# Weights loaded in contiguous parts with a later down load, and two float32 convolutions turned into float32r

## The reference, cut to what matters

```python
y = irfft(rfft(u, n=1024) * rfft(K, n=1024))[..., :512] + u * D[:, None]   # per row and channel
y = y * (arange(512) < length[:, None])
gate_out = fake_quant_linear(y, gate_w)      # 512 -> 1376, input rounded to FP8 e4m3 and back
up_out = fake_quant_linear(y, up_w)          # 512 -> 1376
hidden = silu(gate_out) * up_out
out = x + fake_quant_linear(hidden, down_w)  # 1376 -> 512, hidden rounded to FP8 e4m3 and back
```

## Time and profile before

| what | value |
|---|---|
| median of 3 runs | 311.52 us (311.35 to 312.45) |
| the profiled execution | 311.96 us, of which the trace's span is 310.2 us |
| PE busy | 298.6 us (96% of the span) |
| DVE busy | 216.1 us (70%) |
| ACT busy | 181.4 us (58%) |
| POOL busy | 40.4 us (13%) |
| granted TensorE clock | full in every slice |

### The profile page before, as it was taken

One profiled execution on the slowest core, in us unless ns is written; L12 is line 12 of the kernel. 1 busy time (PEld: TensorE's weight loads), 2 busy tenths in 40 slices (PEclk: granted clock), 3 DMA queues, 4 the chain that ended last, 5 costly groups with the idle time before them and its releaser, 6 DMA issues.

```text
span 310.2 us, 5071 instructions
## 1 busy us (share of the span) xinstructions
PE 298.6 (96%) x1833; PEld 171.1 (55%) x1833; DVE 216.1 (70%) x441; ACT 181.4 (58%) x248; POOL 40.4 (13%) x109
## 2 busy tenths in 40 slices
PE   1999999999999999999999999999999999999995
PEld 0457764755466555755556555655456554644443
DVE  6979699887756886678765886668764857453444
ACT  4926397386655567475755748466663646544640
POOL 4031000031001400022001400014001400140010
PEclk9999999999999999999999999999999999999999
DMA  6879999700705625074613726073001750060028
GB/s 199 194 189 229 298 238 314 294 4 0 270 2 85 188 71 200 2 136 137 227 43 56 190 41 254 0 135 135 3 1 21 150 237 0 10 128 0 2 41 230
DMA packets 14016, 38.43 MB, mean 124 GB/s; under 512 B 1470, under 2 KB 6558, under 8 KB 11052
## 3 DMA queue, kind: packets, MB, share of 16 engines
q1 hardware_dynamic: 8412, 26.61, 24.8%
q0 software_dynamic: 5584, 11.57, 21.5%
HBM read 33.93 MB, written 15.81 MB: 160 GB/s over the span
## 4 chain that ended last, share of the span: by engine, by line
PE 93%; DVE 3%; DMA 2%; issue 0%; SPq 0%
PE gate_ps L670 22%; PE up_ps L670 22%; PE down_ps L593 19%; PE y_ps L577 13%; PE y_ps L558 4%; PE y_ps L573 2%; PE gate_ps L643 2%; PE up_ps L643 2%; PE y_ps L611 2%; PE down_ps L711 2%; PE down_ps L611 2%; PE y_ps L711 1%; DMA toep<-kpad_scratch 1%; DMA prm<-in_params 1%; PE up_ps L623 1%; PE down_ps L517 1%
## 5 line engine op out<-in xcount | busy, mean ns | idle before, releaser
L977 DVE SCALAR_TENSOR_TENSOR hv<-sil,fac,up_ps 128x512 f32<-128x512 f32 (+1 forms) x88 | 64.7, 736 | 76.3 <-PE up_ps L670 44.1
L445 ACT ACTIVATE sil<-gate_ps,fac 128x512 f32<-128x512 f32 (+1 forms) x88 | 59.6, 677 | 97.7 <-PE gate_ps L670 79.5
L670 PE MATMUL gate_ps<-yq,wg 128*128 128x512 bf16 (+3 forms) x344 | 82.3, 362 | 0.0
L670 PE MATMUL up_ps<-yq,wu 128*128 128x512 bf16 (+3 forms) x344 | 82.3, 362 | 0.0
L593 PE MATMUL down_ps<-wd,hq 128*128 128x512 bf16 (+1 forms) x264 | 68.2, 380 | 0.0
L670 PEld LDWEIGHTS up_ps<-yq,wu 128*128 128x128 bf16 (+1 forms) x344 | 32.9, 98 | 35.7
L670 PEld LDWEIGHTS gate_ps<-yq,wg 128*128 128x128 bf16 (+1 forms) x344 | 32.4, 98 | 35.4 <-issue 0.5
L419 ACT ACTIVATE hq<-hv 128x1024 uint16<-128x1024 uint16 (+1 forms) x41 | 42.5, 1037 | 0.0
L410 ACT ACTIVATE yq<-yv 128x1024 uint16<-128x1024 uint16 x32 | 33.6, 1050 | 8.6 <-DVE yv L954 8.6
L577 PE MATMUL y_ps<-xh,th 128*128 128x512 f32 (+2 forms) x78 | 37.3, 478 | 0.6 <-issue 0.6
L593 PEld LDWEIGHTS down_ps<-wd,hq 128*128 128x128 bf16 (+1 forms) x264 | 23.0, 98 | 24.6 <-issue 6.0
(11 more groups left out here) (171 smaller groups left out, 273.9 us busy)
## 6 DMA issues: line engine op xcount, KB each, us to landing
xt<-in_xT SPq DMA_DIRECT2D x8, 1024.0 KB, 4.8
out<-in_x SPq DMA_DIRECT2D x7, 1024.0 KB, 5.3
out<-res POOLq DMA_DIRECT2D x7, 1024.0 KB, 7.7
toep<-kpad_scratch SPq DMA_DIRECT2D x6, 1024.0 KB, 7.5
toep<-kpad_scratch SPq DMA_DIRECT2D x8, 256.0 KB, 4.1
wd<-in_down POOLq DMA_DIRECT2D x1, 1280.0 KB, 18.8
xt<-in_x SPq DMA_DIRECT2D x1, 1024.0 KB, 7.3
out<-xt SPq DMA_DIRECT2D x3, 256.0 KB, 3.8
```

The lines of the kernel that those rows point to most:

```text
L445: nc.scalar.activation(sil[b][0:w, 0:cols], gate_ps[b][0:w, 0:cols], ACT.Silu, scale=fac[0:w, S_GATE:S_GATE + 1]).then_inc(silu_done, 1)
L670: mm = nc.tensor.matmul(ps[b][0:w, cols], wt[:, k, c * P:c * P + w], yq[par][:, version, k, cols], start=(k == 0), stop=(k == LB - 1))
L977: v.scalar_tensor_tensor(hv[c // 2 % 3][0:w, c % 2, 0:cols], sil[b][0:w, 0:cols], fac[0:w, S_UP:S_UP + 1], up_ps[b][0:w, 0:cols], ALU.mult ...
```

## The change

It has two parts. First, the gate and up weights get three tiles each in place of one (`wg[0]` to `wg[2]`), and the arrays in memory are laid out part by part, so that each partition's share of a part is one run: 1024, 1536 or 2944 float32 values in place of four runs of 256, 384 or 736. The down weights are laid out by partition too, so that ten runs of 512 values become one of 5120, and their load waits for block 2's Toeplitz rows (`conv_in[0]`) instead of block 1's fourth channel (`toep_first[7]`). Second, the third and fourth channel of block 0 are convolved by a new function `conv_low_taps_last` in float32r, from the pair of tiles `xh[1]`, `xl[1]`, `th[1]`, `tl[1]`; it takes the products with `tl` last. The casts and subtractions that this needs are put ahead of `code_y` on ACT and around the first `scale_y` on DVE.

```diff
+WEIGHT_PARTS = ((0, EARLY), (EARLY, MIDDLE), (MIDDLE, I))
...
-        wg = sb("wg", [P, LB, I], BF16)
-        wu = sb("wu", [P, LB, I], BF16)
+        wg = [sb(f"wg{i}", [P, LB, hi - lo], BF16) for i, (lo, hi) in enumerate(WEIGHT_PARTS)]
+        wu = [sb(f"wu{i}", [P, LB, hi - lo], BF16) for i, (lo, hi) in enumerate(WEIGHT_PARTS)]
...
+        def load_weights(eng, wt, w_d, i):
+            lo, hi = WEIGHT_PARTS[i]
+            return eng.dma_start(wt[i][:].rearrange("p k n -> p (k n)"), w_d[:, LB * lo:LB * hi])
...
-            pool.dma_start(wg[:, :, MIDDLE:], wg_d[:, :, MIDDLE:]).then_inc(weights_in, 16)
-            pool.dma_start(wu[:, :, MIDDLE:], wu_d[:, :, MIDDLE:]).then_inc(weights_in, 16)
-            pool.wait_ge(toep_first[2 * HB - 1], 16)
-            pool.dma_start(wd[:, 0:CH - 1, :],
-                           wd_d[0:(CH - 1) * P, :].rearrange("(k p) n -> p k n", p=P)).then_inc(down_in, 16)
-            pool.dma_start(wd[0:TAIL, CH - 1, :], wd_d[(CH - 1) * P:I, :]).then_inc(down_in, 16)
+            load_weights(pool, wg, wg_d, 2).then_inc(weights_in, 16)
+            load_weights(pool, wu, wu_d, 2).then_inc(weights_in, 16)
+            pool.wait_ge(conv_in[0], 16)
+            pool.dma_start(wd[:, 0:CH - 1, :].rearrange("p k n -> p (k n)"),
+                           wd_d[:, 0:(CH - 1) * L]).then_inc(down_in, 16)
+            pool.dma_start(wd[0:TAIL, CH - 1, :], wd_d[0:TAIL, (CH - 1) * L:]).then_inc(down_in, 16)
...
+            high_x_first(0, 1)
+            high_taps_first(0, 1)
             code_y(0, 0, 0)
             code_y(0, 0, 1)
             code_y(0, 0, 2)
-            high_x_first(1)
+            high_x_first(1, 1)
             code_y(0, 0, 3)
-            high_taps_first(1)
+            high_taps_first(1, 1)
...
+            def conv_low_taps_last(g, h):
+
+                pair, q = h // 2, h % 2
+                pe.wait_ge(x_split, splits_to(g, pair))
+                pe.wait_ge(taps_high, splits_to(g, pair))
+                pe.wait_ge(yv_done, HB * g + h - 1)
+                for taps, xs in ((th, xh), (th, xl), (toep, xt), (tl, xh)):
+                    if taps is tl:
+                        pe.wait_ge(taps_split, splits_to(g, pair))
+                    for d in (3,) if taps is toep else (0, 1, 2):
+                        cols, rest = slice(d * P, (d + 1) * P), slice(0, L - d * P)
+                        ch = (g, h) if taps is toep else (pair, q)
+                        last = nc.tensor.matmul(y_ps[q][:, d * P:L], taps[ch[0]][:, ch[1], cols], xs[ch[0]][:, ch[1], rest],
+                                                start=(taps is th and xs is xh and d == 0), stop=(taps is tl and d == 2))
+                last.then_inc(y_ready, 1)
...
-            for h in range(HB):
-                conv_whole(0, h)
+            conv_whole(0, 0)
+            conv_whole(0, 1)
+            conv_low_taps_last(0, 2)
+            conv_low_taps_last(0, 3)
             k_of(2)
...
+            low_x(0, 1)
             scale_y(0, 0)
+            low_taps(0, 1)
             scale_y(0, 1)
```

More of the change, by code:

```diff
@@ L200, in at_least, with splits_to @@
                 eng.wait_ge(s, v)
+        def splits_to(g, pair):
+            return 1 if isinstance(g, int) and g == 0 else 2 * (g - 1) + pair + 1
         def k_in_bank(i, half):
@@ L219, in high, with weights_of @@
             return ap.bitcast(U16).rearrange("p a (b s) -> p a b s", s=2)[:, :, :, 1]
+        def weights_of(wt, k, c):
+            i = 0 if c * P < EARLY else 1 if c * P < MIDDLE else 2
+            lo = c * P - WEIGHT_PARTS[i][0]
+            return wt[i][:, k, lo:lo + width(c)]
+        def load_weights(eng, wt, w_d, i):
+            lo, hi = WEIGHT_PARTS[i]
+            return eng.dma_start(wt[i][:].rearrange("p k n -> p (k n)"), w_d[:, LB * lo:LB * hi])
         def yq_of(par, h):
@@ L530, in warm @@
                 for n in range(count):
-                    nc.tensor.matmul(y_ps[n % 2][:], wg[:, 0, 0:P], wg[:, 0:2, 0:EARLY], start=True, stop=True)
+                    nc.tensor.matmul(y_ps[n % 2][:], wg[0][:, 0, 0:P], wg[0][:, 0:2, :], start=True, stop=True)
             pe.wait_ge(unit_in, 32)
@@ L566, in conv @@
                 if distances[0] == 0:
-                    at_least(pe, x_split, 2 * (g - 1) + pair)
-                    at_least(pe, taps_split, 2 * (g - 1) + pair)
+                    at_least(pe, x_split, splits_to(g, pair))
+                    at_least(pe, taps_split, splits_to(g, pair))
                     at_least(pe, yv_done, m - 1)
@@ L622, in by_channel @@
                         for k in range(LB):
-                            mm = nc.tensor.matmul(ps[c][:, cols], wt[:, k, c * P:(c + 1) * P],
+                            mm = nc.tensor.matmul(ps[c][:, cols], weights_of(wt, k, c),
                                                   yq[0][:, version, k, cols], start=(k == 0), stop=(k == LB - 1))
@@ L669, in slots @@
                                 for k in range(LB):
-                                    mm = nc.tensor.matmul(ps[b][0:w, cols], wt[:, k, c * P:c * P + w],
+                                    mm = nc.tensor.matmul(ps[b][0:w, cols], weights_of(wt, k, c),
                                                           yq[par][:, version, k, cols], start=(k == 0), stop=(k == LB - 1))
@@ L1137, in by_k, with by_chunk @@
     def by_k(w):
-        return w.T.reshape(LB, P, I).transpose(1, 0, 2)
+        rows = w.T.reshape(LB, P, I).transpose(1, 0, 2)
+        return np.concatenate([rows[:, :, lo:hi].reshape(P, -1) for lo, hi in WEIGHT_PARTS], axis=1)
+    def by_chunk(w):
+        rows = np.concatenate([w.T, np.zeros((CH * P - I, L), w.dtype)], axis=0)
+        return rows.reshape(CH, P, L).transpose(1, 0, 2).reshape(P, CH * L)
     arrays = {
         "in_xT": xt, "in_x": x, "in_params": params, "in_scales": scales, "in_unit": unit, "in_stepped": stepped,
-        "in_gate": by_k(a["L0_ffn_gate_w"]), "in_up": by_k(a["L0_ffn_up_w"]), "in_down": a["L0_ffn_down_w"].T,
+        "in_gate": by_k(a["L0_ffn_gate_w"]), "in_up": by_k(a["L0_ffn_up_w"]), "in_down": by_chunk(a["L0_ffn_down_w"]),
     }
```

29 lines of the change are left out of this document (15 added, 14 removed).

## The result

The changed kernel takes 312.6 us (median of 20 runs, 311.98 to 314.98). The kernel before, run beside it, takes 312.12 us (20 runs, 311.35 to 312.97). The ratio is 1.0026 [1.0016, 1.0035]: 0.26% slower, about 0.8 us (the medians differ by 0.5). Two of the 20 executions took 314.64 and 314.98 us; none of the kernel before went above 312.97. The forecast of 310.9 us was wrong in sign, and 312.6 lies outside its range of 310.0 to 312.1. Of its miss of 1.7 us, 0.6 is the baseline: the forecast started from three executions with a median of 311.52 us, and twenty give 312.12. The other 1.1 us are the change itself, forecast at -0.65 and measured at +0.5 by the medians. The profiled execution took 313.02 us with a span of 311.2 us, against 311.96 and 310.2 before: 1.0 us more.

What follows compares the result with a forecast made beforehand. PE was taken to bound the kernel: two float32r channels save 0.72 us, less a 0.07 us wait, giving 0.65 off the median of 311.52, so 310.9 us; range 310.0 to 312.1.

Steps and rivals of the forecast that it cites:

- the sum: Block 0's third and fourth channel: float32r pieces add to 1.80 us a channel against 2.16, saving 0.72 us in two.
- change of kind: Float32r matmul behind a float32 one on PE: bare weight load could cost 0 to 0.57 us in all, taken as 0.
- The wait of 0.6 us: PE's wait at 50.74 us for block 2's `low_taps` from DVE: claimed to stay, moving forward with PE.
- rival C: Block 2's x comes earlier, splits move ahead on ACT, the 50.74 us wait goes too: 310.2 us, chance 0.14.
- nearly every microsecond that is taken from PE behind 17.38 us comes off the end: PE from block 0's channels on: time saved reaches the end if inputs are in time; gain forecast 0.65 us.
- can't give PE time by themselves: Loads throughout: no gain of their own, because PE waits for none; `wu`'s last part decides whether 0.65 us comes through.
- second rule: DMA engines take turns between queues packet by packet, so POOL's longer runs would delay block 2's rows and the down weights.
- rival B: Down weights land late at block 1's head, PE waits 1.55 us: 312.4 us, chance 0.12.
- the two edits: Down weights moved behind block 2's rows, and one run per partition: together more than 0.55 us earlier landing of `wu`.
- Rival A: Weights still gate slot 5, where PE waits up to 0.55 us: 311.4 us, chance 0.12.
- Rival B's first rule: GpSimd can't write descriptors during VectorE's two-port operations, so the down weights' later issue would be slower; no size given.

Runs made afterwards that it cites:

- rows_first: Changed kernel with the second and third part of gate and up issued behind block 1's fourth channel instead of block 0's: 315.5 us, ratio 1.0114.
- convs_wait_pieces: Kernel before plus float32r convolutions, later wait for the down weights and 8 warming matmuls cut into 48, short runs: 311.94 us, ratio 0.9998.
- late_in_two: Like convs_wait_pieces, with the third part of gate and up loaded in two, each with its own wait: 311.28 us, 0.9976 against the kernel before.
- after_pieces: Changed kernel, long runs included, with the 8 warming matmuls cut into 48 pieces: 317.76 us, ratio 1.0181.
- before_pieces: Kernel before with the 8 warming matmuls of 512 columns cut into 48 of 96: 312.04 us, ratio 1.0.
- runs_only: Kernel before with only the tiles and long runs of all weights, plain convolutions, down weights still behind block 1's fourth channel: 319.6 us, ratio 1.0233.
- after_fewer_warm: Changed kernel with 2 warming matmuls in place of 8 ahead of K's second part: 313.93 us, ratio 1.0061.

## Why the prediction was wrong

**Right.** Float32r saves 0.66 us in two channels (0.65 forecast), in part by luck. The first group of three float32r matmuls behind a float32 one took 0.71 us (21.76 to 22.47) where the sum had 0.53, so one change of kind did lie bare, with 0.18 us, and the prediction had put all of them at 0. The float32 piece of 128 columns, at 0.14 us (22.99 to 23.13) for 0.22, and a first pair of channels of 4.24 us for 4.32 covered it. The casts and subtractions fit into ACT's and DVE's idle time, with `scale_y` at 22.18 as worked out. The down weights come without a wait; they were issued 3.5 us later than forecast, since block 2's rows were later. The wait of 0.6 us stays, and rival C (it goes) did not come. Slot 5 has no wait in the changed kernel, since `wu` lands at 21.36 + 17.4 = 38.8 us.

**The first step that failed:** "nearly every microsecond that is taken from PE behind 17.38 us comes off the end". The trace of before had the counter-evidence, 0.27 us of idle PEld inside a group of four that waited for nothing, and I read only PE's waits, where it isn't listed. The new convolutions moved a stop six matmuls forward, and all the changed kernel's gain went into it: 1.96 us against 0.27. That its place hangs on the count is shown: it stands behind the 23rd matmul in all five kernels that have the new convolutions, the 8 warming matmuls and a stop, and behind the 29th in the three without the convolutions and in the one with six warming matmuls fewer. That its length hangs on the load of the DMA queues is shown by `rows_first`, where it goes with the load alone. That PE waits for the packet of instructions is the reading that fits both, and it is inferred.

**The second:** the loads "can't give PE time by themselves". True for a gain; I didn't ask for a loss at block 1's rows. In the kernel before the cast of `th` ends at 30.81 us, and with DVE's 0.95 us behind it `tl` can be there at about 31.8, some 4.1 us ahead of PE's need at 35.88. The long runs took 4.75 (29.98 to 34.73) and left `tl` 0.7 us too late. The prediction had the mechanism, as the second rule under rival B, but followed it only to block 2's rows and the down weights. The first rows in that queue are block 1's, which land while `wu` travels. Priced there, B's mechanism would have had another place and a threshold of 4.1 us of delay in rows that take 5.8 us to land.

**The third, in the sum:** the two edits that should bring `wu` 0.55 us earlier. The later wait brings nothing (22.2 us for 22.4). The long runs bring 5 us, ten times what was needed, and it is these 5 us that SP's queue paid. Rival A (slot 5 gates) was seen with the convolutions and short runs, but only once the stop was gone: 1.0 us in an execution whose weights were issued late, and about 0.7 us by the ratios of `convs_wait_pieces` and `late_in_two` (0.9998 and 0.9976), whose intervals overlap a little.

**Rival B's first rule**, that GpSimd's descriptors are held up by VectorE (the Trainium skill, "SBUF — State Buffer", section "SBUF: two separate sides"), stays untested. The large down transfer was issued in 0.53 us at 41.03, beside one DVE operation (0.75 us from 41.15), and landed 9.1 us later, without a delay; whether that operation was in a two-port mode the trace doesn't say.

**What stays open.** When exactly PE asks for its instructions, so that the stop's length could be forecast; why block 1's rows are later still in `after_pieces`; why block 0's fourth Toeplitz channel is late in two of the kernels with pieces; how much of the convolutions' 0.65 us reaches the end when nothing else is in the way; and why the changed kernel is 0.26 us quicker behind the tail slot.

## What to carry to other kernels

Before a gain on the critical engine is counted to the end, look in its stretch for gaps that no semaphore explains ("issue" on PE or PEld in the middle of a group), and count instructions to them: work that is made of more instructions moves such a stop, and where it then falls decides how long it is. Longer runs were no free gain here, where two queues share the DMA engines: as the bytes per packet of one queue grew, the other queue's share fell, and the first thing to check is the slack of every load in that other queue. Where several limits lie within a microsecond of each other, removing one shows the next; here, of all kernels tried, only the two without stop, with short runs and with the third part of the weights in two (with and without the float32r convolutions) were faster than the kernel before.

## What the runs showed of the hardware

- Packets of 0.02 MB on a queue of their own, which the profile calls the instruction queue, go through the DMA engines. The first behind 17 us went with a stop of PE of 0.3 to 1.8 us where it came among data packets near the channel-by-channel stretch (27.0 to 29.7 us); over nearly idle queues (`rows_first`), or in a stretch of long float32 matmuls (`before_pieces`), it went with none. The second, between 29.9 and 35.7 us, went with none either.
- Two queues took turns packet by packet where POOL's runs were long (274 to 270 packets from 28 to 36 us), and nearly so where they were short (515 to 448 from 30 to 36 us, but 1009 to 281 from 24 to 30).
- A PE that had idled was slower for a while. Behind 4.86 us of idle time the granted clock was 0.57 over 52 to 56 us (`runs_only`); behind 4.62 us it was 0.50, its lower level of 1.2 GHz, over 40 to 44 us (`after_pieces`). In `after_fewer_warm`, behind 2.1 us of idle time, the granted clock was recorded as full, and still two channels took 6.40 us in place of 4.58.
